# A graph layer on one core: left rows first, then right rows and keys, with the first 32 gathers in the front

## The reference

```
xn = layernorm(x)
# graph attention, 4 heads of 64
xl = xn @ W_l;  xr = xn @ W_r
e = leaky_relu(xl[src] + xr[dst], 0.2)
score = einsum('ehd,hd->eh', e, att)
alpha = softmax of score over the edges of one dst
agg = segment_sum(alpha * xl[src], dst)
gnn = layernorm(elu(agg + bias) + xn) * gamma + beta
# lambda mix
sm = softmax(xn @ W_k + b_k, over all nodes)
lam = sm.T @ (xn @ W_v + b_v);  mix = (xn @ W_q + b_q) @ norm(lam)
x = x + gnn + mix
# then top-1 mixture of 8 experts on layernorm(x), added to x
```

## Time and profile before

| | us |
|---|---|
| median of the runs | 1357.16 (1356.49 to 1357.85) |
| the profiled execution, its own time | 1358.6 |
| its span | 1356.7 |
| busy PE / DVE / ACT / POOL | 1133.4 / 1073.8 / 835.8 / 821.7 |
| share of the span | 84% / 79% / 62% / 61% |
| mean granted clock of PE | 0.931 of full speed |

### The profile page before, as it was taken

The page is one execution under the profiler, slowest core; times in us unless marked ns, Lnnn a source line. Parts: engine busy times, 40 slices in busy tenths (PEclk is TensorE's granted clock), DMA queues, the critical chain, the costliest instruction groups (busy, mean ns, idle before and its releaser), DMA issues. The chain is left out here.

```text
span 1356.7 us, 24446 instructions
## 1 busy us (share of the span) xinstructions
PE 1133.4 (84%) x5685; PEld 835.1 (62%) x5685; DVE 1073.8 (79%) x2305; ACT 835.8 (62%) x3252; POOL 821.7 (61%) x849
## 2 busy tenths in 40 slices
PE   7959698989888889888898888888877562999994
PEld 4537576767666666667666676666655452565652
DVE  5956889999989999998998999999984882053535
ACT  1531279788889877788887888988774321323230
POOL 5217777777777777777777777777743634022133
PEclk9988999989999999999999999999999665999997
DMA  5566678878888877787887887788712444336320
GB/s 165 207 229 192 172 188 211 198 194 207 209 200 208 207 195 195 205 207 201 204 209 187 206 206 207 206 200 203 190 51 71 127 140 149 104 96 176 100 85 16
DMA packets 162621, 234.91 MB, mean 173 GB/s; under 512 B 40085, under 2 KB 131490, under 8 KB 161747
## 3 DMA queue, kind: packets, MB, share of 16 engines
q1 hardware_dynamic: 118434, 127.66, 33.8%
q0 software_dynamic: 41216, 103.67, 30.8%
q10 hardware_dynamic: 2880, 2.66, 0.6%
HBM read 187.01 MB, written 48.91 MB: 174 GB/s over the span
## 5 line engine op out<-in xcount | busy, mean ns | idle before, releaser
L1456 ACT ACTIVATE e_prod<-gathered_rows,e_prod 128x64 f32<-128x64 f32 x2728 | 670.3, 334 | 5.7
L1010 POOL DMA_INDIRECT gathered_rows<-d_xl,e_idx x576 | 549.6, 954 | 175.5 <-issue 161.8
L1400 PE MATMUL bank<-e_prod,e_selt 128*128 128x260 f32 x1408 | 361.1, 402 | 41.4 <-DVE e_acc L1127 19.5
L1400 PEld LDWEIGHTS bank<-e_prod,e_selt 128*128 128x128 f32 x1408 | 271.4, 198 | 93.2 <-issue 44.9
L1346 PE MATMUL bank<-e_xr,e_sel 128*128 128x256 bf16 x2112 | 296.9, 278 | 2.0 <-issue 0.3
L1351 PE MATMUL bank<-gathered_rows,ident 128*128 128x256 f32 x704 | 220.4, 395 | 45.7 <-DMA gathered_rows<-d_xl,e_idx 29.3
L1346 PEld LDWEIGHTS bank<-e_xr,e_sel 128*128 128x128 bf16 x2112 | 207.9, 100 | 75.5 <-issue 11.0
L1105 DVE TENSOR_REDUCE e_score<-e_edge 128x16 f32<-128x1024 f32 x176 | 213.1, 1211 | 0.3
L1010 POOL DMA_INDIRECT gathered_rows<-d_xl,src_cols x128 | 122.9, 960 | 71.7 <-issue 36.8
L1351 PEld LDWEIGHTS bank<-gathered_rows,ident 128*128 128x128 f32 x704 | 108.0, 194 | 67.4 <-DMA gathered_rows<-d_xl,e_idx 45.0
L1895 POOL DMA_INDIRECT out_dram<-f_out,f_index x32 | 45.2, 1413 | 161.0 <-DVE f_out L2010 156.2
(11 more groups left out here) (314 smaller groups left out, 1105.9 us busy)
## 6 DMA issues: line engine op xcount, KB each, us to landing
e_xr<-d_xr SPq DMA_DIRECT2D x176, 192.0 KB
d_hist<-e_acc SPq DMA_DIRECT2D x176, 130.0 KB
e_drow<-d_rel SPq DMA_DIRECT2D x176, 128.0 KB
w_rows<-in_L_ffn_w_dram SPq DMA_DIRECT2D x16, 1024.0 KB, 7.1
gathered_rows<-d_xl,e_idx POOLq DMA_INDIRECT x576
d_in<-zero SPq DMA_DIRECT2D x6, 1032.0 KB, 4.7
e_rows<-d_rows SPq DMA_DIRECT2D x22, 192.5 KB
d_xr<-a_xr SPq DMA_DIRECT2D x20, 192.0 KB, 1.9
```

What stands on the lines that cost most here:

```text
L1010: pool.indirect_dma_start(xl[:, q.slot * G + g, :], None, m.d_xl, bass.IndirectOffsetOnAxis(ap=column, axis=0)).then_inc(gathered[q.slot], 16)
L1400: last = pe.matmul(ps_agg[b], selt[:, b, g, :], flat(prod[:, b, g, :, :]), start=(g == 0), stop=(g == G - 1))
L1456: last = act.activation(prod[:, b, g, h, 0:HEAD], xl[:, q.slot * G + g, h * HEAD:h * HEAD + HEAD], ACT.Copy, scale=prod[:, b, g, h, HEAD:H ...
```

## The change

In the front all left rows are made first (`left_product`, 20 tiles), then all right rows and keys (`right_product`). DVE does its statistics and normal rows at once, ahead of its part of the right rows. PE gets two banks for turned rows, two for left and four for right products. When all left rows are stored, POOL issues the first 32 gathers (quads 0 to 7, `first_rows`) still in the front; attention's POOL then starts at quad 8, without the wait for `ctxps`. To free the ring, the keys lie in the rows of x, and the lambda weights have memory of their own. x is loaded again from its input by SP at the end of attention (`reload`), and POOL's additions wait for it. The tops of the keys and the row that is subtracted are made at the end of the front; the subtraction itself is cut in five, one piece behind each of quads 0 to 4, and the context sums move from behind quads 1 to 5 to behind quads 2 to 6. SP's loads for quads 0 to 3 are issued at the end of the front. The tables of `walks` become bf16, with 12 small matmuls for 18. The edge tables go to DRAM at other tiles.

```
-KEYS_AT = RING * G // 2
+EARLY = RING // 2
...
+    m.keys = m.x
+    m.w_q = sb("lambda_w_q", [P, 2, DIM])[:, :, :]
...
-                if n == 15:
+                if n == 8:
                     sp.wait_ge(s["tables"], 1)
                     sp.dma_start(m.d_rel.rearrange("(c p) e -> p c e", p=P), rel16[:, :, :]).then_inc(s["stored"], 16)
-                if n == 18:
+                if n == 14:
                     sp.wait_ge(s["tables"], 2)
...
+            for r in range(4):
+                sp.wait_ge(stored_r[r], 16)
+            sp.wait_ge(s["stored"], 32)
+            settle(sp, m)
+            for k in range(4):
+                base = sp.value_load(m.base[0:1, k:k + 1], min_val=0, max_val=LAST_BASE)
+                sp.dma_start(m.drow[:, k, :], ...).then_inc(m.loaded[k], 16)
+                sp.dma_start(m.xr[:, k, :], m.d_xr[bass.ds(base * SPAN, P), :]).then_inc(m.loaded[k], 16)
...
+            def first_rows():
+                pool.wait_ge(s["taken"], 2)
+                for r in range(4):
+                    pool.wait_ge(stored_l[r], 16 * FOURS)
+                settle(pool, m)
+                for i in range(EARLY * G):
+                    pool.indirect_dma_start(m.ring[:, i, :], None, m.d_xl, bass.IndirectOffsetOnAxis(
+                        ap=m.idx[:, i:i + 1], axis=0)).then_inc(m.gathered[i // G], 16)
...
+            def left_product(n):
+                pe.wait_ge(s["xt"], n + 1)
+                if n >= 2:
+                    pe.wait_ge(s["xl"], n - 1)
...
+            def right_product(n):
+                if n == 0:
+                    pe.wait_ge(s["xt"], TILES)
+                    pe.wait_ge(s["xl"], TILES)
+                if n >= 4:
+                    pe.wait_ge(s["rest"], n - 3)
+                    pe.wait_ge(s["keys"], n - 3)
...
+            def reload(b):
+                tiles = slice(4 * b, min(4 * b + 4, TILES - 1))
+                if b == 0:
+                    sp.wait_ge(sl["ctxps"], 1)
+                sp.dma_start(m.x[:, tiles, :], ...).then_inc(sl["x"], 16)
...
+                if q.known() and QUADS <= q.k < QUADS + FOURS:
+                    reload(q.k - QUADS)
...
-                if q.known() and q.k == RUN:
-                    pool.wait_ge(sl["ctxps"], 1)
...
+                if q.known() and q.k < EARLY:
+                    return
                 if q.since(RING):
                     pool.wait_ge(s["prod"], q.k - RING + 1)
...
+            pool.wait_ge(sl["x"], 16 * (FOURS + 1))
...
-                if q.known() and q.k == RUN - 1:
+                if q.known() and q.k < FOURS:
+                    keys_less(q.k)
+                if q.known() and q.k == RUN:
                     lambda_rows()
...
-                    if 1 <= q.k <= FOURS:
-                        contexts(q.k - 1)
+                    if 2 <= q.k <= FOURS + 1:
+                        contexts(q.k - 2)
```

More of the change, by code:

```diff
@@ L164, in memory @@
     m.met = ctx.enter_context(nc.semaphore("met"))
+    m.loaded = [ctx.enter_context(nc.semaphore(f"att_loaded{r}")) for r in range(4)]
+    m.gathered = [ctx.enter_context(nc.semaphore(f"att_gathered{r}")) for r in range(RING)]
+    m.shifted = ctx.enter_context(nc.semaphore("lam_shifted"))
     m.d_xl = dram("d_xl", (PAD, ROW))
@@ L239, in survey @@
     s = sem_set(nc, m.front, "sur", "ends att blank ones ident tri ids iotas later zeros half var rstd xn aug chain "
-                "wa scaled norm fixed endsps passed walkps places shifts gathered links shiftps turned turnps taken linksps tables stored "
-                "xtps xt right left hi keys rest mid xr xl peak")
+                "wa scaled norm fixed endsps passed walkps places shifts gathered fetched links shiftps turned turnps taken linksps tables stored "
+                "xtps xt right left hi keys rest mid xr xl peak base pair maxps peaks top topps bottom")
     FOURS = TILES // 4
@@ L768, in products @@
                 pe.wait_ge(s["xt"], n + 1)
                 if n >= 2:
[L770 to L771 removed]
+                    pe.wait_ge(s["xl"], n - 1)
                 for h in range(2):
[L773 removed]
+                    last = pe.matmul(ps_l[n % 2][:, 0:ROW], m.xnt[:, n, h * P:h * P + P], w_l[:, h, :], start=(h == 0), stop=(h == 1))
@@ new lines, in left_product @@
+                last.then_inc(s["left"], 1)
+            def right_product(n):
[5 more added lines that the diff above has]
+                    pe.wait_ge(s["keys"], n - 3)
+                for h in range(2):
+                    last = pe.matmul(ps_rk[n % 4][:, :], m.xnt[:, n, h * P:h * P + P], w_rk[:, h, :, :].rearrange("p k c -> p (k c)"),
@@ L794, in _ @@
                 if n == 12:
                     turn_sources()
-                if n == 16:
+                if n + 2 < TILES:
+                    turn_rows(n + 2)
+            pe.wait_ge(weights[1], 64)
+            for n in range(TILES):
+                right_product(n)
+                if n == 6:
+                    shifts()
+                if n == 10:
+                    turn_lanes()
+                if n == 13:
                     next_joins()
                 if n == 17:
-                    turn_lanes()
@@ L1275, in _ @@
         def _(pe):
-            def key_tops():
-                for half in range(2):
-                    last = pe.transpose(ps_max[:, half * P:half * P + P], m.key_max[:, half * P:half * P + P], m.ident[:, :])
-                last.then_inc(sl["maxps"], 1)
-                pe.wait_ge(sl["top"], 1)
-                for half in range(2):
-                    last = pe.matmul(ps_top[:, half * P:half * P + P], mx[:, half:half + 1], m.ident[:, :], start=True, stop=True)
-                last.then_inc(sl["topps"], 1)
-                pe.wait_ge(sl["shift"], 1)
-                pe.matmul(ps_shift, m.ones[0:1, :], shift[:, :], start=True, stop=True).then_inc(sl["shiftps"], 1)
             def contexts(b):
```

334 lines of the change are left out of this document (174 added, 160 removed).

## The result

The changed kernel takes 1354.89 us (median of 18 runs, 1352.41 to 1362.03) against 1357.13 of the kernel before, run beside it (18 runs, 1352.82 to 1363.25): a ratio of 0.9978, 95% interval 0.9968 to 0.9989, so 1.5 to 4.3 us are won. The forecast was 1344 us; the measured time lies above the range (1335 to 1353).

A forecast was written before the change was run, and what follows sets the result against it. The prediction took POOL's gathers to bound attention, so quad 16's start and the closing tail decide. Quad 16 15.0 us earlier and 2.0 us more tail gave -13.0 us: 1344 us from 1357.16, range 1335 to 1353.

The forecast's parts named there:

- What bounds the kernel: Attention loop: POOL's gathers are full at 5.04 us a quad, so quad 16's start and the closing tail set attention's end.
- Part 1: Front: full DMA engines set the start of attention on the engines (T0) at 98.7, ends 94.5 and 103; before, 96.5.
- By PE and SP alone: Front: without the DMA term, PE's products, last stores and four loads would let attention start near 95.5.
- the same 3 us: Front's end: attention starts 3 us after the DMA engines run dry, as in the kernel before, here after 95.7.
- Part 2: Attention's start to quad 16: POOL waits until quad 0 is weighed, 66.7 us after the start; quad 16 15.0 us earlier.
- Part 3: Attention's loop: POOL's time unchanged, 160 quads of 5.04 us; DVE catches up after five of twenty runs.
- Part 4: Attention's tail: reloading x and POOL's later additions beside DVE's closing quads add 2 us (0 to 4).
- A: Front: DMA doesn't bind, attention starts at 95.5, the kernel takes 1341 us; chance 0.25.
- B: Loop: the consumers, not POOL, become the bound; only the lead of 7 us remains, 1352 us; chance 0.15.
- C: Right stage: DMA falls to attention's rate, 249 GB/s when full, attention starts at 113, 1359 us; chance 0.05.
- D: Front: DVE locks POOL out, gathers take 2.2 us instead of 1.26, attention starts at 120, 1365 us; chance 0.02.
- E: Front: left rows land past 67 instead of 43, attention starts at 108 to 112, nothing measurable gained; chance 0.04.

The follow-up runs named there:

- f1_fills_tail: The changed kernel with the zero blocks for the expert inputs stored in attention's closing tail, not in the front: 1343.29 us, ratio to the kernel before 0.9884.
- f3_twelve: The changed kernel with only 12 gathers in the front, the other 20 at the start of attention: 1351.07 us, ratio to the kernel before 0.9939.
- i1_all: The changed kernel with zero blocks in the tail, loads of quads 0 to 3 behind tiles 10 to 13, row added by PE, x reloaded at quads 164 to 168: 1351.80 us.
- j1_split: The changed kernel with zero blocks in the tail, x reloaded at quads 164 to 168, POOL's last two additions later, 20 front gathers: 1337.92 us.
- h2_pe_adds: The changed kernel with the row added by PE in the node update instead of POOL's five additions: 1711.14 us, ratio 1.0012, on a chip where PE pauses.

## Why the prediction was wrong, step by step

**What bounds the kernel**: right. POOL bounds the loop at 5.04 us a quad; all that counts is when quad 16 begins and what the tail takes. In f1_fills_tail quad 16 began 18 us earlier than before and the last gather 17.9.

**Part 1, T0 = 98.7: wrong, this is the step that failed.** Measured 105.8, past the end of 103. The pieces: left rows landed at 48.6 (46), POOL's gathers done at 91.5 (87), hidden. PE was done with the right products at 83.5 (81). "By PE and SP alone" 95.5 is near the 95.2 of f1_fills_tail, but by luck: there the last right rows go out at 85.6 (84), the loads are issued by 93.5 (90.5), and attention begins 1.7 us behind them, where the forecast had 5. "This binds, not PE" was right as well: the engines were full until about 98 (95.7). Wrong was the join: to the DMA sum I added "the same 3 us" of the kernel before and left the four loads out, as if they ran beside the full engines. They could not. SP issues the last right rows only when ACT has a buffer for them, and ACT's buffer comes free with a landing, so the last store is itself issued near the end of the full stretch (96.16) and not at 84; links, loads and the meeting take 9.7 us behind it. It had to be a sum, 96 + 9.7, not a maximum. Counted from the dry engines, 98 to 105.8 is 7.8 us and not 3, which is 4.8 of the 7.1 us; f1_fills_tail and f3_twelve show the stretch behind the links unchanged (9.2 and 9.3) while its start moves by 10.5 and 5.2. The other 2.3 us are the end of the full stretch, 98 for 95.7. The engine time itself came out: from 53.5 to 98 SP's queue held 67.7% of the engines and POOL's 27.2%, together 42.2 us for the forecast's 42.1. But the engines were not full from 53.5, only from 64 (0.67 between), which cost 3 us. On the rule of the Trainium skill, page "DMA: Bandwidth & Descriptors", section "Issuing engines are not separate DMA queues": f3_twelve agrees that moved gathers are paid for in the stores' time, with 0.26 us each for the 0.50 that I had from the row of attention. By its queue's share a gather held the engines for 0.40 us here (12.1 us for some 30), so the share overstates what leaving it out wins.

**Part 2, weighed at T0 + 66.7: right**, measured 66.6 (172.4), then the gather at 173.17. The first context product came at T0 + 13.1, exactly as summed. The other 2.5 us were forecast as 2.4, half of PE's waits for rows, and the halving was a guess. POOL's idle time was forecast as a single wait of 25 us for ACT. It was two: 13.0 for the lambda variance, whose root stands behind the 64th gather in POOL's list, and 13.0 for ACT. The first cost nothing here, as the second ended last.

**Part 3, the loop: right.** 805.0 us, no further wait for ACT over 0.8 us. PE's waits for gathered rows are absent from 150 to 250 us (8.6 us in the kernel before) and from 250 to 350 are back at 1.2 (1.4 before).

**Part 4, tail + 2 (0 to 4): too small**, + 4.7. That POOL's additions would hit DVE was right, where they hit was not. I took two or three hits of DVE's shares at 1.3 us. But it was the chain of small operations that was hit, five times and 8.3 us, of which 4.3 were lost on balance. Another 1.4 went in the closing quads, and nearly 1 came back ahead of the chain. The waiting for the reload (11.7 us) was forecast as 11.

**The rivals.** A (T0 95.5) fell with T0, though f1_fills_tail has just that T0. B (consumers bind) did not happen: POOL waits for issue only. C fell: full engines moved 379 to 422 GB/s, not 249; its idea that ACT waits for store buffers is true, 16.1 us. D fell: gathers in the front took 1.04 us on the mean, 1.73 at most. E is nearest in T0 and in the time, but by another way: the left rows were there at 48.6, not at 67.

The sum with the measured terms: 7.6 us earlier at quad 16, 7.5 at the last gather, less 4.7 in the tail, 2.8 at the node update. The stages behind it took 322.2 us before, 320.2 after and 317.7 to 322.6 in the other runs without pauses, unchanged but for i1_all; so 2 us of the span's 4.8 belong to no step and lie within what these stages differ by from one trace to the next.

## What to carry to other kernels

When a buffer ring couples a producer to full DMA engines, as here, the last store leaves at the end of the full stretch, and everything that the issuing engine does behind it is added: take the sum of the two, not the larger. List every chain that hangs on the last store's data (here the key maxima too), for it is the next bound once the first is moved. Look for large transfers with a late due time (here 6.3 MB of zeros, needed a millisecond later) and move them to a stretch where the engines idle. And before moving a POOL operation, list which DVE operations will run beside it: in this trace small ones in a chain were hit each for the rest of the POOL operation, whatever their own size. Then look for waits in the same chain that the longer operations will hide.

## What the runs showed of the hardware

A DVE operation of 1 partition by 4 values took 1.32 us beside a POOL addition of 2.5, and 0.15 without; a tensor_scalar of that size 2.27 against 0.16. One that reads the PSUM bank beside SBUF (L1236, 0.38) kept its length, and one with two SBUF operands (L1244, 0.27) slipped between two additions. The Trainium skill, page "SBUF — State Buffer", section "SBUF: two separate sides", has it that a port pair shared by DVE and GpSimd is locked for a whole instruction, and that the loser blocks fully; these lengths agree, and the 12.5 us of the five additions, 11.8 before, fit a POOL that was held a little too.

Stores and row gathers together kept 16 engines at 379 to 422 GB/s, more than the 367 of the stores before and far from the 204 of attention (249 when full). A gather cost 0.26 to 0.31 us of the stores' time at full engines (f3_twelve), and about 0.1, not clear of nothing, at engines with room (j1_split).

A matmul with one partition of height took as long as one of 128 (both 256 columns: 565 and 559 ns a record, i1_all).

On two of the chips PE paused with nothing to wait for in the profile; the same kernel took 27% longer there (1724 against 1357). The longest pause that the profile lays to no engine is 12.78 us, in the front of h2_pe_adds (L799); there ACT and DVE stood too, ACT took up PE's last product 10.1 us after its recorded end, and the operation of DVE that L799 needs had ended just before it. Whether PE or its signals were held, and why these chips do so, stays open.
